# Dispatch of a soft mixture of experts: the shares taken as a second exponential, and all four batches contracted as high and low parts

## What is computed

```python
logits = jnp.einsum('bmd,dnp->bmnp', x, phi)            # b 4, m 1024, d 256, n 64 experts x p 32 slots
dispatch = jax.nn.softmax(logits, axis=0)               # over the four batches
combine = jax.nn.softmax(logits.reshape(bsz, m, n * p), axis=-1)
slots = jnp.einsum('bmd,bmnp->bnpd', x, dispatch)
y = jnp.einsum('bnpd,nde->bnpe', slots, W) + b
out = jnp.einsum('bnpd,bmnp->bmd', y, combine)
```

## Time and profile before

| | |
|---|---|
| median of 3 runs | 1467.93 us (1466.76 to 1469.3) |
| profiled execution, span from first to last instruction | 1465.5 us |
| busy: PE, PE weight loads | 1373.6 us (94%), 1212.6 us (83%) |
| busy: DVE, ACT, POOL | 889.3 (61%), 658.5 (45%), 749.0 us (51%) |
| mean granted TensorE clock | 0.971 |

### The profile page before, as it was taken

One profiled execution on the slowest core, in us unless ns is written; L12 is line 12 of the kernel. 1 busy time (PEld: TensorE's weight loads), 2 busy tenths in 40 slices (PEclk: granted clock), 3 DMA queues, 4 the chain that ended last, 5 costly groups with the idle time before them and its releaser, 6 DMA issues. The chain is left out here.

```text
span 1465.5 us, 29372 instructions
## 1 busy us (share of the span) xinstructions
PE 1373.6 (94%) x9361; PEld 1212.6 (83%) x9362; DVE 889.3 (61%) x1869; ACT 658.5 (45%) x1206; POOL 749.0 (51%) x693
## 2 busy tenths in 40 slices
PE   7997798999999995899988999999999998999998
PEld 3454687888888884677778999999999988999997
DVE  5787522332332333677578888888888864566656
ACT  4553432333333331666544444444444435555553
POOL 6663187765550002331039887987987957240400
PEclk9997799999999998899999999999999999999999
DMA  4111425232220002310033274474474587465450
GB/s 169 48 43 56 151 65 176 100 117 100 85 97 14 14 15 92 113 58 1 1 116 88 80 208 119 146 208 119 146 208 116 148 252 265 159 216 187 151 206 30
DMA packets 112543, 171.49 MB, mean 117 GB/s; under 512 B 6400, under 2 KB 97664, under 8 KB 106336
## 3 DMA queue, kind: packets, MB, share of 16 engines
q1 hardware_dynamic: 103456, 156.27, 33.1%
q0 software_dynamic: 3408, 9.31, 2.2%
q10 hardware_dynamic: 5616, 5.11, 1.0%
HBM read 115.22 MB, written 55.44 MB: 116 GB/s over the span
## 5 line engine op out<-in xcount | busy, mean ns | idle before, releaser
L2109 PE MATMUL comb_psO<-hand_parts,comb_eh 128*128 (+1 forms) x1024 | 198.7, 292 | 0.5 <-DVE comb_el L2228 0.3
L1774 ACT ACTIVATE disp_raw<-disp_psL 128x512 f32<-128x512 f32 x128 | 76.6, 598 | 198.7 <-PE disp_psL L1686 112.1
L2109 PEld LDWEIGHTS comb_psO<-hand_parts,comb_eh 128*128 128x128 f32 x1024 | 157.5, 190 | 1.1 <-DVE comb_el L2228 0.7
L1087 DVE TENSOR_TENSOR moe_hs<-moe_psH,moe_act_a 128x512 f32<-128x512 f32 x78 | 50.3, 686 | 178.0 <-PE moe_psH L981 144.1
L1686 PE MATMUL disp_psL<-disp_ph,hand_xh 128*128 (+1 forms) x512 | 147.8, 289 | 0.8 <-DVE disp_e L1959 0.8
L1686 PE MATMUL disp_psL<-disp_ph,hand_xl 128*128 (+1 forms) x512 | 145.0, 283 | 0.0
L1686 PE MATMUL disp_psL<-disp_pl,hand_xh 128*128 (+1 forms) x512 | 144.9, 283 | 0.0
L2109 PE MATMUL comb_psO<-hand_parts,comb_el 128*128 (+1 forms) x512 | 144.6, 282 | 0.0
L2228 DVE TENSOR_TENSOR comb_el<-comb_psT,comb_eh 128x512 fp32r<-128x512 f32 x128 | 88.0, 689 | 91.3 <-ACT comb_eh L2143 88.8
L1710 PE MATMUL disp_psS<-disp_e,last_x 128*128 128x256 f32 x512 | 132.8, 382 | 3.8 <-POOL disp_e L1868 3.8
L1185 POOL DMA_INDIRECT lin_yg<-sorted_y,table_place x32 | 32.5, 1015 | 191.4 <-POOLq L896 143.3
(11 more groups left out here) (287 smaller groups left out, 3919.6 us busy)
## 6 DMA issues: line engine op xcount, KB each, us to landing
logits<-disp_raw SPq DMA_DIRECT2D x64, 512.0 KB, 4.0
hand_e<-logits SPq DMA_DIRECT2D x32, 1024.0 KB, 6.3
w_raw<-in_w SPq DMA_DIRECT2D x8, 2048.0 KB
disp_wt<-in_w_slot SPq DMA_DIRECT2D x16, 1024.0 KB, 9.9
w_raw<-in_w SPq DMA_DIRECT2D x8, 1024.0 KB
slot_y<-disp_slots SPq DMA_DIRECT2D x64, 128.0 KB, 3.2
disp_bt<-in_b_slot SPq DMA_DIRECT2D x15, 512.0 KB, 4.9
comb_y_in<-slot_y SPq DMA_DIRECT2D x3, 2048.0 KB, 10.5
```

What stands on the lines that cost most here:

```text
L1087: v.tensor_tensor(hs[:, cols], psH[:, 2 + h, :], act_a[:, cols], ALU.mult).then_inc(hs_ready, 1)
L1774: nc.scalar.activation(raw[mc % 4][:, half * 2:half * 2 + 2, :], psL[l_bank[mc]][:, half * 2:half * 2 + 2, :], ACT.Copy).then_inc(copied, 1)
L2109: last = nc.tensor.matmul(psO[j % 2][:, 0:D], ep[s % EB][:, i, :], yp[:, bass.ds(odd, 1), ch * D:(ch + 1) * D].rearrange("p a d -> p (a d) ...
```

## The change

The reciprocal and the two multiplications by it go. In their place ACT takes the logarithm of the sum in place (`log_of_sum`), DVE subtracts it from the (logit less maximum) of all four batches (`power`, one instruction on 128x1024), and ACT takes the exponential again (`share`); the first exponential goes to a tile of its own (`first_exp`). `high_of_share` and the low part now cover four batches, in two halves, batches 2 and 3 first (the low part is `low_of_share`). `contract` makes three fp32r products for every batch. `eh` gets four copies that lie over `raw`, so `first_half` waits for the contraction of step g-4 too, and `high_of_share` waits for the stored logits and for `peak`. x is split for all 32 tiles: `natural_high` for batches 0 to 2 in the stage before, for batch 3 in two instructions in `dispatch`. The bias load is issued ahead of the stores, and the late peaks take their place in the steps.

```diff
-SPLIT_B = 2
+SPLIT_B = 4
+EARLY_B = 3
...
-            for t in range(SPLIT_B * TB):
+            for t in range(EARLY_B * TB):
                 natural_high(t)
...
-                wait(pe, share_ready, g + 1)
+                wait(pe, part_ready, 2 * g + 1)
...
-                        if b >= SPLIT_B:
-                            products = ((x, e[mc % 4]),)
-                        else:
-                            products = ((natural, eh[mc % 2]), (natural, el[mc % 4]), (natural_lo, eh[mc % 2]))
-                        if kd == 0 and b == SPLIT_B - 1:
+                        products = ((natural, eh[mc % 4]), (natural, el[mc % 4]), (natural_lo, eh[mc % 4]))
+                        if kd == 0 and b == B // 2 - 1:
                             wait(pe, part_ready, 2 * g + 2)
...
+            def log_of_sum(g, mc):
+                wait(act, sum_ready, g + 1)
+                nc.scalar.activation(rs[mc % 2][:], rs[mc % 2][:], ACT.Ln).then_inc(log_ready, 1)
+
+            def share(g, mc):
+                wait(act, power_ready, g + 1)
+                nc.scalar.activation(e[mc % 4], e[mc % 4], ACT.Exp).then_inc(share_ready, 1)
+
+            def high_of_share(k, g, mc):
+                wait(act, share_ready, g + 1)
+                wait(act, kept[mc % 4], k * (MC // 4 * 16) + (mc // 4 + 1) * 16)
+                wait(act, peaked, g + 1)
+                for h in (1, 0):
+                    nc.scalar.activation(eh[mc % 4][:, h * 2:h * 2 + 2, :], e[mc % 4][:, h * 2:h * 2 + 2, :], ACT.Copy).then_inc(eh_ready, 1)
...
             def exponent(g, mc):
                 wait(act, less, 2 * g + 2)
-                nc.scalar.activation(e[mc % 4], e[mc % 4], ACT.Exp).then_inc(exp_ready, 1)
+                wait(act, sum_ready, g)
+                nc.scalar.activation(first_exp[:], e[mc % 4], ACT.Exp).then_inc(exp_ready, 1)
...
-            def share(g, mc):
-                wait(pool, rsum_ready, g + 1)
...
+            def low_of_share(g, mc):
+                for n, h in enumerate((1, 0)):
+                    wait(pool, eh_ready, 2 * g + (n + 1))
+                    nc.gpsimd.tensor_tensor(el[mc % 4][:, h * 2:h * 2 + 2, :], e[mc % 4][:, h * 2:h * 2 + 2, :],
+                                            eh[mc % 4][:, h * 2:h * 2 + 2, :].bitcast(F32), ALU.subtract).then_inc(part_ready, 1)
...
-            def invert(g, mc):
-                wait(dve, sum_ready, g + 1)
-                v.reciprocal(rs[mc % 2][:], rs[mc % 2][:]).then_inc(rsum_ready, 1)
+            def power(g, mc):
+                wait(dve, log_ready, g + 1)
+                v.tensor_tensor(e[mc % 4], e[mc % 4], rs[mc % 2][:].unsqueeze(1).to_broadcast([P, B, BLK]),
+                                ALU.subtract).then_inc(power_ready, 1)
```

More of the change, by code:

```diff
@@ L1645, in _ @@
                         h = y_step[mc - 1]
-                        store(k - 1, last[h], h)
-                        load_bias(last[1] if h == 0 else here)
+                        store(k - 1, last[h], h, last[1] if h == 0 else here)
                 load(here)
@@ L1799, in step @@
                 first_half(k, g, mc)
+                if mc >= EH_LAG or not fresh:
+                    share(g - EH_LAG, (mc - EH_LAG) % MC)
                 second_half(g, mc)
-                if mc >= EH_LAG or not fresh:
-                    high_of_share(g - EH_LAG, (mc - EH_LAG) % MC)
+                if mc >= 1 or not fresh:
+                    log_of_sum(g - 1, (mc - 1) % MC)
                 if mc == SPLIT_AT:
                     high_of_phi(k + 1, after)
+                if mc >= EH_LAG or not fresh:
+                    kb, mb = before(k, mc, EH_LAG)
+                    high_of_share(kb, g - EH_LAG, mb)
+                exponent(g, mc)
                 if mc == EVAC and not fresh:
@@ L1807, in step @@
                     evacuate(0)
-                exponent(g, mc)
-                if mc == EVAC and not fresh:
                     evacuate(1)
@@ L1841, in _ @@
                     step(k, mc, bass.ds(other, 1))
-            for mc in range(MC - EH_LAG, MC):
-                high_of_share((NBLK - 1) * MC + mc, mc)
+            last = NBLK * MC - 1
+            share(last - 1, MC - 2)
+            high_of_share(NBLK - 1, last - 1, MC - 2)
+            log_of_sum(last, MC - 1)
+            share(last, MC - 1)
+            high_of_share(NBLK - 1, last, MC - 1)
             act.wait_ge(half_summed, 1)
@@ L1877, in step @@
-                wait(pool, sum_ready, g)
-                nc.gpsimd.tensor_tensor(s2[:], e[mc % 4][:, 0:2, :], e[mc % 4][:, 2:4, :], ALU.add).then_inc(pair_sum, 1)
-                wait(pool, pair_sum, g + 1)
-                nc.gpsimd.tensor_tensor(rs[mc % 2][:], s2[:, 0, :], s2[:, 1, :], ALU.add).then_inc(sum_ready, 1)
-                if mc > 0 or not fresh:
-                    share(g - 1, (mc - 1) % MC)
-            for j in range(5):
+                add_up(g, mc)
+                if mc > 0 or not fresh:
+                    low_of_share(g - 1, (mc - 1) % MC)
@@ L1885, in _ @@
+            half = TB // LATE_HIGHS
+            for t in range(EARLY_B * TB, B * TB, half):
+                nc.gpsimd.tensor_copy(natural[:, t:t + half, :], x[:, t:t + half, :]).then_inc(natural_low, 1)
+            for j in range(4):
                 natural_rest(j)
             step(0, 0, fresh=True)
-            for j in range(5, 7):
+            for j in range(4, 6):
                 natural_rest(j)
             step(0, 1, fresh=True)
+            natural_rest(6)
+            step(0, 2, fresh=True)
@@ L1890, in _ @@
             natural_rest(7)
-            for mc in range(2, MC):
+            for mc in range(3, MC):
                 step(0, mc, fresh=True)
@@ L1941, in peak, with step @@
                                 raw[mc % 4][:], X, ALU.max).then_inc(peaked, 1)
-            def step(k, mc, after, fresh=False, ending=False, late=False):
+            def step(k, mc, after, fresh=False, ending=False):
                 g = k * MC + mc
@@ L1960, in step @@
                 if mc > 0 or not fresh:
-                    invert(g - 1, (mc - 1) % MC)
+                    power(g - 1, (mc - 1) % MC)
                 if ending:
                     last_sum(g, mc)
-                    invert(g, mc)
                 if mc == SPLIT_AT:
                     low_of_phi(k + 1, after)
-                if not late:
-                    peak(k, mc)
+                peak(k, mc)
+                if ending:
+                    power(g, mc)
             for n in range(0, 3):
@@ L1987, in _ @@
             for mc in range(MC):
-                step(NBLK - 1, mc, slice(0, 1), ending=mc == MC - 1, late=mc >= MC - LATE_PEAKS)
-            for mc in range(MC - LATE_PEAKS, MC):
-                peak(NBLK - 1, mc)
+                step(NBLK - 1, mc, slice(0, 1), ending=mc == MC - 1)
             wait(dve, peaked, NBLK * MC)
```

65 lines of the change are left out of this document (35 added, 30 removed).

## The result

The changed kernel takes 1484.91 us (median of 4 runs, 1480.81 to 1488.81) against 1467.35 us before on the same chip: a ratio of 1.0118, 95% interval 1.0103 to 1.0133. The forecast was 1480 us with a range of 1458 to 1491. The sign and the mechanism hold. The 5 us that are missing in the forecast are the rest of a larger miss in the loop, most of it from a place that it had costed at nothing, and of gains elsewhere that it didn't foresee either.

A forecast was written before the change was run, and what follows sets the result against it. PE bound dispatch before; after the change a 6.14 us ring would. Start 4.9, rest of block 1 0.5, six blocks of 0.85 (5.1) and end 1.5 make +12.0 on 1467.9: 1480 us, range 1458 to 1491.

The forecast's parts named there:

- PE saves 2.3 us a block: Dispatch: three products replace each float32 matmul, a step falls from 6.02 to 5.74 us, a block to 52.8.
- The ring: Dispatch loop: sum, logarithm, rounding, low part, next sum across ACT and POOL, DVE's subtraction holding POOL; 6.14 us a step.
- The six waits: PE's six contractions up to the next experts wait 0.6, 0.35, 0.4, 0.4, 0.6, 0.75 us; sum 3.1 a block.
- the sign of being right: Blocks 1 to 7: first copies of mc 7 to 3 lie 6.1 apart, PE waits 0.3 to 0.8 in six contractions.
- A block of 55.9: Dispatch block: 52.8 us plus 3.1 of waits, in place of 55.07, +0.85 us a block.
- The earlier bias load frees DVE, which PE didn't wait for: Dispatch loop: issuing the bias load earlier was listed as costing nothing.
- The start, +4.9: Up to step 7's contraction: POOL's pieces of x take some 21 us in place of 11; contraction ends at 826.6, before 821.7.
- The end, +1.5: Behind step 63: the chain from sum to low part puts the last product at T+17.8, before T+15.98.
- Costing nothing: Spare ACT and DVE time, covered casts, combine's additions, table load, rounding's waits and earlier bias load: no cost expected.
- DVE not holding POOL (1459 us): Rival 1: DVE doesn't hold POOL in the ring; ring 5.7, block near 53.3, 1459 us; chance 0.15.
- Balance (1465 to 1471): Rival 2: PE's savings and waits balance, each wait 0.3 shorter than read; 1465 to 1471 us; chance 0.12.
- A longer ring (1486 to 1491): Rival 3: DVE holds POOL to its end or longer, ACT's rounding late; ring 6.28 to 6.4; chance 0.15.

The follow-up runs named there:

- the kernel without late transfers: Changed kernel with the bias load and stores of y issued ahead of the logits store on SP; 1477.02 us, ratio 1.0080 to the kernel before.
- the maximum: Kernel with bias and y ahead of the logits store, DVE's subtraction of the logarithm replaced by a maximum over the same tile; 1449.51 us, ratio 0.9877.
- the second exponential alone: Changed kernel's new share, but batches 2 and 3 contracted in float32, one low part a step, no further natural parts; 1464.95 us, ratio 0.9997.
- the second profile: The changed kernel itself, unaltered, run again beside the kernel before on another chip; 1481.66 us, ratio 1.0105.
- the roundings ahead: Changed kernel with ACT's two roundings of the share of step g-2 ahead of the logarithm of step g-1; 1464.10 us, ratio 1.0012.
- both reorderings: Changed kernel with roundings ahead of the logarithm on ACT, and bias and y ahead of the logits store on SP; 1458.28 us, ratio 0.9954.
- POOL's pieces moved: Kernel with both of those orders changed, plus piece 4 of x's low parts ahead of the first sum, later pieces earlier; 1458.73 us, ratio 0.9938.

## Why the prediction held, and where it didn't

- **PE saves 2.3 us a block.** Right. With nothing in PE's way a block is 52.87, forecast 52.8.
- **The ring.** Right. In the kernel without late transfers, first copies of steps 0, 1 and 2 lie 6.06 to 6.11 us apart, forecast 6.14. POOL's pair is 0.5 longer in the ring (3.06 against 2.55), which is the 1.54 against 1.05 us behind the sum that the forecast read. The interpolated 1.19 us for DVE's subtraction was 1.22, 2.2 where POOL was first (forecast 2 to 2.4). The subtraction's turn between POOL's two low parts behind the experts was right as well. The logarithm took 0.42, the bound that was chosen. Opening the ring on ACT gave what the reading implies; taking the exclusion away gave more, a block of 52.87 where 53.9 to 54.4 was expected.
- **The six waits.** Their sum is right, the single ones less so. Without late transfers a block is 3.24 us over the one with the maximum, forecast 3.1. But it isn't 6.1 from step to step throughout, as the sign of being right says: first copies of steps 2 and 3 lie 7.25 apart, those of 3 and 4 only 5.28. PE's booked waits in a block are 0.2 to 0.3 us at five contractions and 0.7 at one, and each hides another 0.16.
- **A block of 55.9.** The ring's part was 56.11, 0.2 too low. The block of the changed kernel was 57.07. The step that failed is "The earlier bias load frees DVE, which PE didn't wait for". Two transfers, the bias and the stores of y, reach PE by DVE and by ACT's wait at L1833, which the forecast didn't name at all. They cost 0.96 us a block, 5.8 us over six blocks. DVE's wait for the bias had been seen as harmless, and it is harmless in a loop where POOL and DVE have slack to PE, as before the change and in the run with the second exponential alone. In the ring, with the bias behind the stores as before, a wait of 3.5 us and more cost 1.3. ACT's wait for the stores is another thing: the earlier bias load brings it, and it costs without a ring too. The earlier issue of the bias is still worth its place: without it the change would stand at 1.0152.
- **Luck in the total.** From T(0,0) to T(7,7) the profiled execution lost 18.6 us, forecast 10.2 (the start with the rest of block 1, and six blocks, less the 0.3 by which step 63 comes sooner). The 8.4 that are missing are about 5.8 from the transfers, 1.2 from the ring's 0.2 a block, and 1.3 from the start. Against them stand 3.1 us ahead of T(0,0), which no part of the forecast is about and the second profile doesn't show, and 2.35 behind the last product, where the end itself took 0.5 more than forecast. So the span was missed by 3.5 us only, because errors of both signs met; the median is 3.9 us above its span where 2.4 was assumed, which makes the 5.
- **The start, +4.9.** Mis-sized. Step 7's contraction ends at 824.77 in the changed kernel, 71.6 us behind T(0,0); before it was 821.7 and 65.4. That is +6.2. POOL's pieces of x were read well: the last ends 30.6 us behind T(0,0), forecast 30.7, and the sum of step 3 ends at 32.6, forecast 32.9. The further 1.3 us come behind it, in the five rings from the sum of step 3 to that of step 8, which take 32.6 us in place of the 31.1 that the forecast has; the longest of them is 7.3, and why was not looked into. That POOL's work is the cause fits two runs: without the second low part and the further natural parts it is +0.3 to T(1,3), and filling POOL's idle time in front of the first sum gives 1.75 back.
- **The end, +1.5.** The last product starts at T + 18.18 and so ends at T + 18.3; the forecast's 17.8, like its 15.98 before, is such an end. The line of the table is +2.3 where the forecast has +1.8. In the second profile of the changed kernel it is +1.8 (the last product at T + 17.62). Against it the stage behind gained 2.35 (2.45 in the second profile), where the forecast had 0. The rows for both stand in the last section.
- **Costing nothing.** One table load, and four more additions of 2.4 us in combine, which didn't get longer by them: right. ACT's order of the evacuations had no effect either, but that was tried with the ring open alone; whether it makes the fifth and sixth waits larger in the closed ring stays open.
- **The rivals.** DVE not holding POOL (1459 us) would have come with steps of 5.7; the run with the maximum shows what it would have been, 1449.5 on its chip, as there a block is 52.87 and not the 53.3 that the rival gives. Balance (1465 to 1471) would need each wait 0.3 shorter; they sum to 3.24 us a block, as read. A longer ring (1486 to 1491) is the one that the time came near to, but its mechanism, POOL held to DVE's very end, is not what happened.

## What to carry to other kernels

Before work is moved off the bound engine, count what the loop between the helpers takes from one sum to the next, in the order in which each engine issues: an instruction placed ahead of another on ACT made a loop of 6.1 us out of 4.6 us of work, and swapping two lines was worth 2.1 us a block. When a loop turns from "bound by one engine" to "bound by a ring", waits that were hidden have to be costed again: DVE's wait for the bias cost nothing before and 1.3 us a block in the ring. Moving a load ahead of stores has a price of its own, paid by whoever waits for the stores. And for POOL and DVE add up the time of those instructions that exclude each other: here DVE's with two SBUF tiles as inputs, and a `tensor_scalar`, not its reciprocals or maxima.

## What the runs showed of the hardware

**The exclusion between DVE and POOL goes instruction by instruction.** With POOL first at 913.92, DVE's subtraction began at 914.09 and took 2.22 us; of the pair the first low part took 1.30 as alone and the second 2.28, so DVE ran between them; the pair took 3.54, its 2.55 alone and 1 us for DVE. With DVE first (920.02 to 921.24), POOL's pair ended at 923.65, so it ran from about 921.10, 0.14 us ahead of DVE's end, as in the earlier trace rows. DVE's `tensor_scalar`, with one SBUF input and an output of the same size, collided in the same way (0.68 alone, 1.68), the maximum, with one input and four elements of output, not at all. It isn't the output's size that decides: the reciprocal of the kernel before has one SBUF input and an output as large as it; it takes 1.74 to 1.75 us in all 64 steps, and POOL's instructions beside it keep their distance of 1.26.

**Transfers beside others take longer to land.** The same 512 KB of bias landed 6.1 us behind its issue (median) with the logits store issued 0.7 us ahead of it, and 4.2 us when it went first. A store of y landed after 5.1 us behind the bias load and the logits store, after 3.1 behind the logits store alone, and after 3.3 behind the bias load alone.

**The clock at the end.** In the changed kernel PE waits 2.53 us for POOL's low part at 1208.84, behind a wait of 1.24 at 1203.93, and 0.71 again at 1210.53; from there it runs slowly:

```profile
1208.84 0.39 PE L1711 MATMUL disp_psS<-disp_eh,last_natural 128*128 128x256 f32 x1 [2.53 <-POOL disp_el L1903]
...
1210.53 0.58 PE L1711 MATMUL disp_psS<-disp_eh,last_natural 128*128 128x256 f32 x1 [0.71 <-POOL disp_el L1903]
```

In the windows of both kernels (busy time of PE, PEld, DVE, ACT, POOL, then the granted clock), first the changed one, then the one before, where the slow stretch comes later, at the beginning of combine:

```profile
1208.80:1210.50 1.70, 0.98 (x6) 0.78 (x6) 1.67 (x2) 1.67 (x3) 1.70 (x2) 1.00 1.05 153
1210.50:1213.90 3.40, 3.37 (x16) 3.38 (x17) 3.37 (x5) 1.28 (x3) 3.40 (x2) 0.51 1.06 294
1213.90:1220.00 6.10, 6.10 (x52) 6.03 (x51) 0.30 (x1) 2.44 (x5) 2.81 (x3) 1.00 1.05 387
```

```profile
1217.70:1222.30 4.60, 4.19 (x23) 3.82 (x24) 1.55 (x3) 3.55 (x5) 4.41 (x4) 0.63 0.74 272
1222.30:1230.00 7.70, 7.48 (x64) 7.27 (x63) 4.92 (x6) 4.79 (x7) 7.70 (x4) 1.00 0.92 346
```

0.51 is the lower level, 1.2 GHz. 16 products take 3.4 us there, which at 0.12 us each are 1.9. PE then runs through to the last product, so these 1.5 us are a part of the 2.3 that the end got longer. In the kernel before, 0.63 over 4.6 us would be 1.7 us lost, behind the last product; the changed kernel has no such stretch there (1.00 between 1234.90 and 1240.00), and combine gained 2.35.

The slow stretch is not bound to come in one place or the other. In four profiles (the roundings ahead, the maximum, the second exponential alone, both reorderings) it comes in neither, and from the last product to the span's end they take 260.6 to 261.9 us, like the changed kernel's 261.1. Nor does it always cost: with POOL's pieces moved, 3.4 us at 1.2 GHz lie ahead of the last product, and it starts at T + 16.05, against T + 16.01 in the kernel with both reorderings, which has none.
